# A four-layer graph network on one core: weight splitting regrouped and moved, and a finer alternation in the last stage

## The reference

```
x = layernorm(x + L0(x, edge_attr, src, dst))   # edge MLP: tanh(concat(x[s], x[r]) @ W0 + b0), tanh(. @ W1 + b1),
                                                # . @ W2 + b2, times (edge_attr @ Wg), mean over the edges of s
x = layernorm(x + L1(x, edge_index))            # two GCN convolutions with self loops, relu between them
x = layernorm(x + L2(x, edge_index))            # three SAGE convolutions, relu between them
x = layernorm(x + L3(x, edge_index))            # mean over neighbours of x @ W + b
```

## Time and profile before

| what | value |
|---|---|
| median of 3 runs | 3159.2 us (3157.09 to 3163.51) |
| the profiled execution's own time | 3163.51 us |
| its span, first to last instruction | 3161.9 us |
| mean granted TensorE clock | 0.988 of full speed |
| PE busy | 3050.7 us (96%) |
| DVE, ACT, POOL busy | 2156.2, 1558.9, 1372.1 us |

### The profile page before, as it was taken

The page is one execution under the profiler, slowest core; times in us unless marked ns, Lnnn a source line. Parts: engine busy times, 40 slices in busy tenths (PEclk is TensorE's granted clock), DMA queues, the critical chain, the costliest instruction groups (busy, mean ns, idle before and its releaser), DMA issues. The chain is left out here.

```text
span 3161.9 us, 65361 instructions
## 1 busy us (share of the span) xinstructions
PE 3050.7 (96%) x17338; PEld 2445.7 (77%) x17340; DVE 2156.2 (68%) x5608; ACT 1558.9 (49%) x3158; POOL 1372.1 (43%) x1479
## 2 busy tenths in 40 slices
PE   7699999999999999999998889999999999999899
PEld 7588888888888888888886566667777888887676
DVE  7788888888888888888885777774655222246523
ACT  2466666666666666666664777771111111111344
POOL 2677777777777777777773211220000000000011
PEclk9899999999999999999999999999999999999999
DMA  5555555555555555555553888887556777778586
GB/s 175 170 164 162 161 165 164 164 164 162 162 164 164 164 164 163 165 163 164 164 163 117 262 262 267 276 276 234 171 183 192 231 220 225 218 231 260 99 127 99
DMA packets 298299, 584.82 MB, mean 185 GB/s; under 512 B 43361, under 2 KB 150842, under 8 KB 298234
## 3 DMA queue, kind: packets, MB, share of 16 engines
q1 hardware_dynamic: 180960, 280.20, 29.9%
q0 software_dynamic: 90416, 254.46, 29.2%
q10 hardware_dynamic: 26858, 49.32, 4.3%
HBM read 493.97 MB, written 110.32 MB: 191 GB/s over the span
## 5 line engine op out<-in xcount | busy, mean ns | idle before, releaser
L985 PE MATMUL bank<-parts,ring 128*128 128x512 f32 x2500 | 622.6, 398 | 4.0 <-DVE T_buf L1761 1.9
L985 PEld LDWEIGHTS bank<-parts,ring 128*128 128x128 f32 x2500 | 461.1, 189 | 104.7 <-issue 5.4
L620 POOL DMA_INDIRECT msgs<-rows_out,sidx x416 | 408.4, 982 | 152.0 <-issue 94.8
L613 POOL DMA_INDIRECT p_in<-p_tab,gidx x416 | 403.4, 970 | 138.7 <-issue 112.7
L613 POOL DMA_INDIRECT q_in<-q_tab,gidx x416 | 398.3, 958 | 126.8 <-issue 126.2
L675 PE MATMUL bank<-hidden1h,w1h 128*108 128x512 f32 x936 | 406.8, 435 | 2.3 <-DVE hidden2l L865 2.3
L675 PE MATMUL bank<-w2h,hidden2h 108*128 108x256 f32 x1248 | 402.1, 322 | 0.0
L676 PE MATMUL bank<-hidden1l,w1h 128*108 128x512 f32 x936 | 369.0, 394 | 0.0
L677 PE MATMUL bank<-hidden1h,w1l 128*108 128x512 f32 x936 | 367.7, 393 | 0.0
L784 ACT ACTIVATE hidden2h<-bank,b1c 108x512 fp32r<-108x512 f32 (+1 forms) x312 | 214.5, 688 | 297.8 <-PE bank L691 297.8
L677 PE MATMUL bank<-w2h,hidden2l 108*128 108x256 f32 x1248 | 351.0, 281 | 0.0
(11 more groups left out here) (253 smaller groups left out, 5858.3 us busy)
## 6 DMA issues: line engine op xcount, KB each, us to landing
ring<-counts SPq DMA_DIRECT2D x500, 320.0 KB, 3.4
R_buf<-msgs SPq DMA_DIRECT2D x544, 130.0 KB, 3.1
counts<-cells ACTq DMA_DIRECT2D x125, 320.0 KB, 3.3
eT<-in_edge_T SPq DMA_DIRECT2D x104, 256.0 KB, 2.9
R_buf<-counts POOLq DMA_DIRECT2D x25, 480.0 KB, 6.8
R_buf<-counts POOLq DMA_DIRECT2D x25, 320.0 KB, 5.8
p_in<-p_tab,gidx POOLq DMA_INDIRECT x416, 3.2
q_in<-q_tab,gidx POOLq DMA_INDIRECT x416, 3.2
```

Source lines behind the costliest of these rows:

```text
L613: pool.indirect_dma_start(out=rows_in[:, z, c], out_offset=None, in_=tab[:], in_offset=bass.IndirectOffsetOnAxis(ap=gidx[:, z, which, c:c ...
L620: pool.indirect_dma_start(out=msgs[:], in_=rows_out[:, z, c], in_offset=None, out_offset=bass.IndirectOffsetOnAxis(ap=sidx[:, z, c:c + 1], ...
L985: mm = pe.matmul(bU[t].rearrange("p (w c) -> p w c", w=2), ring[:, cell(odd, a), t * P:(t + 1) * P].bitcast(dt), parts[k % 2][:, :, a].bit ...
```

## The change

It has five parts.

- **W0 is split in one piece.** ACT makes one cast of 128 by 1664 in place of four of 128 by 416, and DVE one subtraction in place of four; DVE no longer has steps of the index chain between them, and TensorE waits for the whole of it ahead of its first matmul.
- **ACT issues the seven loads of W1, W2, Wg and b1 first**, ahead of its wait for W0, where they stood behind the cast of W0 and the rounding of the first two tiles of x.
- **The low parts of W1 and W2** are made on POOL in the table stage, one third behind `xl` of each of tiles 8, 9 and 10 (six instructions), and the 32-row piece of W1 on DVE after tile 15; DVE's three instructions at the head of the edge stage go.
- **TensorE's wait on `s_one`** ahead of its edge loop goes.
- **The last stage alternates one group of turns with one group of products**, where it alternated two with two.

```diff
--- before.py
+++ after.py
@@ -224,6 +224,7 @@
 
                 @block.tensor
                 def _(pe):
+                    pe.wait_ge(s_w0l, 1)
                     pe.wait_ge(s_cg, 5)
 
                     def totals(n):
@@ -259,8 +260,6 @@
                         for half in range(2):
                             for k in range(KD):
                                 to, q = psum[2 * (n % 3) + half][:, 0:H1], 2 * half + k
-                                if n == 0:
-                                    pe.wait_ge(s_w0l, q + 1)
                                 xk_h, xk_l = xh[:, n % 3, k].bitcast(F32R), xl[:, n % 3, k].bitcast(F32R)
                                 pe.matmul(to, xk_h, w0h[:, q].bitcast(F32R), start=(k == 0), stop=False)
                                 pe.matmul(to, xk_h, w0l[:, q].bitcast(F32R), start=False, stop=False)
@@ -296,18 +295,6 @@
 
                 @block.scalar
                 def _(act):
-                    def round_x(n):
-                        act.wait_ge(s_xt[n % TB], 16 * (n // TB + 1))
-                        wait(act, s_pq, n - 2)
-                        wait(act, s_xl, n - 2)
-                        act.copy(xh[:, n % 3].bitcast(F32R), xt[:, n % TB]).then_inc(s_xh, 1)
-
-                    act.wait_ge(s_w, 32)
-                    for q in range(2 * KD):
-                        act.copy(w0h[:, q].bitcast(F32R), w0[:, q]).then_inc(s_w0h, 1)
-                        if q == 0:
-                            round_x(0)
-                    round_x(1)
                     act.dma_start(w1[:, 0:H1F], W1[0:H1F * P, :].rearrange("(k p) n -> p k n", p=P)).then_inc(s_wl, 16)
                     for i in range(3):
                         act.dma_start(w1[i * H1R:(i + 1) * H1R, H1F], W1[H1F * P:H1, :]).then_inc(s_wl, 16)
@@ -315,6 +302,16 @@
                     act.dma_start(wg[:], Wg).then_inc(s_wl, 16)
                     act.dma_start(b1c[:], b1).then_inc(s_wl, 16)
 
+                    def round_x(n):
+                        act.wait_ge(s_xt[n % TB], 16 * (n // TB + 1))
+                        wait(act, s_pq, n - 2)
+                        wait(act, s_xl, n - 2)
+                        act.copy(xh[:, n % 3].bitcast(F32R), xt[:, n % TB]).then_inc(s_xh, 1)
+
+                    act.wait_ge(s_w, 32)
+                    act.copy(w0h[:].bitcast(F32R), w0[:]).then_inc(s_w0h, 1)
+                    round_x(0)
+                    round_x(1)
                     for n in range(T):
                         j = n % TB
                         if n + 2 < T:
@@ -343,11 +340,20 @@
                     pool.iota(iota_s[:], [[1, NST]], base=0, channel_multiplier=0,
                               allow_small_or_imprecise_dtypes=True).then_inc(s_cg, 1)
                     pool.memset(inert[:], -1.0).then_inc(s_cg, 1)
+                    def weights_low(k):
+
+                        pool.wait_ge(s_hi, 3)
+                        stand_alone(pool, s_up)
+                        pool.tensor_tensor(w1l[:, k].bitcast(F32R), w1[:, k], w1h[:, k], ALU.subtract)
+                        pool.tensor_tensor(w2l[:, k].bitcast(F32R), w2[:, k], w2h[:, k], ALU.subtract)
+
                     for n in range(T):
                         pool.wait_ge(s_xh, n + 1)
                         wait(pool, s_pq, n - 2)
                         pool.tensor_tensor(xl[:, n % 3].bitcast(F32R), xt[:, n % TB], xh[:, n % 3], ALU.subtract
                                            ).then_inc(s_xl, 1)
+                        if TB + 3 <= n < TB + 3 + H1F:
+                            weights_low(n - TB - 3)
                     pool.wait_ge(s_cg, 7)
                     pool.wait_ge(s_xl, T)
 
@@ -375,18 +381,10 @@
 
                     ch.link(v.tensor_scalar(qi[:], xf[:], 1.0 / T, -0.48, ALU.mult, ALU.add))
                     ch.link(v.tensor_copy(qf[:], qi[:]))
-
-                    def w0_low(q):
-
-                        v.wait_ge(s_w0h, q + 1)
-                        v.tensor_tensor(w0l[:, q].bitcast(F32R), w0[:, q], w0h[:, q], ALU.subtract).then_inc(s_w0l, 1)
-
-                    w0_low(0)
+                    v.wait_ge(s_w0h, 1)
+                    v.tensor_tensor(w0l[:].bitcast(F32R), w0[:], w0h[:], ALU.subtract).then_inc(s_w0l, 1)
                     ch.link(v.scalar_tensor_tensor(rf[:], qf[:], -float(T), xf[:], ALU.mult, ALU.add))
-                    w0_low(1)
                     ch.link(v.tensor_scalar(mf[:], rf[:], float(T), None, ALU.is_ge))
-                    w0_low(2)
-                    w0_low(3)
                     ch.link(v.tensor_tensor(qf[:], qf[:], mf[:], ALU.add))
                     ch.link(v.scalar_tensor_tensor(rf[:], mf[:], -float(T), rf[:], ALU.mult, ALU.add))
                     ch.link(v.tensor_scalar(mf[:], rf[:], 0.0, None, ALU.is_lt))
@@ -526,6 +524,10 @@
                             shifted(n)
                         if LATE < n < LATE + HN - 2 and (n - LATE) % 2 == 1:
                             record((n - LATE) // 2)
+                        if n == LATE + HN - 2:
+                            mid = slice(H1R, 2 * H1R)
+                            v.wait_ge(s_hi, 3)
+                            v.tensor_tensor(w1h[mid, H1F].bitcast(F32R), w1[mid, H1F], w1h[mid, H1F], ALU.subtract)
                         if n == AT_ROWS:
                             bucket_rows()
                         if n == AT_COLS:
@@ -734,8 +736,6 @@
                     pe.wait_ge(s_took, j + 1)
                     add_to_ranks(t, rest_b, isinstance(j, int) and j == G - 1).then_inc(s_next, 1)
 
-                pe.wait_ge(s_one, 3)
-
                 def body(t):
                     transposes(t, 0)
                     transposes(t, 1)
@@ -923,16 +923,8 @@
                     message(t, 2)
                     message(t, 3)
 
-                def weights_low():
-
-                    mid = slice(H1R, 2 * H1R)
-                    v.tensor_tensor(w1l[:, 0:H1F].bitcast(F32R), w1[:, 0:H1F], w1h[:, 0:H1F], ALU.subtract)
-                    v.tensor_tensor(w1h[mid, H1F].bitcast(F32R), w1[mid, H1F], w1h[mid, H1F], ALU.subtract)
-                    v.tensor_tensor(w2l[:].bitcast(F32R), w2[:], w2h[:], ALU.subtract)
-
                 for z in range(2):
                     table_rows(z, z)
-                weights_low()
                 v.memset(hidden2h[:], 1.0).then_inc(s_one, 1)
                 v.memset(hidden2l[:], 0.0).then_inc(s_one, 1)
                 v.tensor_copy(count_to, iota[:, 0:P]).then_inc(s_one, 1)
@@ -1573,13 +1565,11 @@
                                 tile_step(3, B - 1, *step)
 
                         def body(n, z, use, turns=True, before=range(QN)):
-                            for lead in range(0, QN, 2):
-                                pair = range(lead, min(lead + 2, QN))
-                                for q in pair if turns else []:
+                            for q in range(QN):
+                                if turns:
                                     turn(n, z, use, q)
-                                for q in pair:
-                                    if q in before:
-                                        products(n - 1, 1 - z, q, AT_exact[1 - z], F32R)
+                                if q in before:
+                                    products(n - 1, 1 - z, q, AT_exact[1 - z], F32R)
 
                         left = range(EARLY, QN)
                         body(1, 1, 0, False, left)
```

More of the change, by code:

```diff
@@ L298, in _ @@
                 def _(act):
+                    act.dma_start(w1[:, 0:H1F], W1[0:H1F * P, :].rearrange("(k p) n -> p k n", p=P)).then_inc(s_wl, 16)
+                    for i in range(3):
+                        act.dma_start(w1[i * H1R:(i + 1) * H1R, H1F], W1[H1F * P:H1, :]).then_inc(s_wl, 16)
+                    act.dma_start(w2[:], W2b.rearrange("(k p) n -> p k n", p=H2P)).then_inc(s_wl, 16)
+                    act.dma_start(wg[:], Wg).then_inc(s_wl, 16)
+                    act.dma_start(b1c[:], b1).then_inc(s_wl, 16)
                     def round_x(n):
@@ L305, in _ @@
                     act.wait_ge(s_w, 32)
-                    for q in range(2 * KD):
-                        act.copy(w0h[:, q].bitcast(F32R), w0[:, q]).then_inc(s_w0h, 1)
-                        if q == 0:
-                            round_x(0)
+                    act.copy(w0h[:].bitcast(F32R), w0[:]).then_inc(s_w0h, 1)
+                    round_x(0)
                     round_x(1)
-                    act.dma_start(w1[:, 0:H1F], W1[0:H1F * P, :].rearrange("(k p) n -> p k n", p=P)).then_inc(s_wl, 16)
-                    for i in range(3):
-                        act.dma_start(w1[i * H1R:(i + 1) * H1R, H1F], W1[H1F * P:H1, :]).then_inc(s_wl, 16)
-                    act.dma_start(w2[:], W2b.rearrange("(k p) n -> p k n", p=H2P)).then_inc(s_wl, 16)
-                    act.dma_start(wg[:], Wg).then_inc(s_wl, 16)
-                    act.dma_start(b1c[:], b1).then_inc(s_wl, 16)
                     for n in range(T):
```

## The result

The changed kernel takes 3172.61 us in the median of 6 runs (3168.55 to 3200.93), the kernel before 3156.88 us in 6 runs beside it (3153.74 to 3163.51). The ratio is 1.0054 with a 95% interval of 1.0031 to 1.0078: slower by 15.7 us as the medians stand, by 17 (10 to 25) as the ratio does. The profiled execution took 3170.52 us, its span is 3168.8.

The account below looks back on a forecast made before the run. DVE was taken to bound the table stage up to 30 us, TensorE the last stage. 1.0 + 2.5 + 2.5 + 0.2 + 0 + 4.7 + 0.9 = 11.8 us on 3159.2 gave 3171.0, range 3163 to 3178.

Parts of the forecast that it names:

- W0 in one piece: Table stage start: undivided cast and subtraction make DVE's chain net 1.0 us later, bounds 0 and 1.6.
- loads first: Kernel start: the seven loads, 1.09 MB, compete with W0's transfer and cost 2.5 us, bounds 0 and 3.3.
- low parts on POOL, and the 32-row piece: Table stage: POOL's six instructions hold up DVE's one-hots, 2.5 us (0 to 4.8); the DVE piece adds 0.2 (0 to 0.5).
- head of the edge stage, `s_one`: Edge stage: DVE's saved 2.6 us are off the path, and TensorE's next adds wait behind the same signal; both 0.
- changes of kind in the last stage: Last stage: three more switches between turns and products per row tile, 0.071 us each over 22 tiles, 4.7 us.
- wait on ACT's copy: Last stage: first products nearly wait for ACT's copy of the last group; 0.04 us a tile, 0.9 in all, bounds 0 and 2.
- early terms absorbed: Start and table stage: loads yield to W0, POOL's instructions fall into spare time; 5.9 us stay, 3165.1; chance 0.15.
- The rival that made the kernel faster by it: Edge stage head: DVE's saved 2.6 us show in full, other terms come to nothing; 3156.6 us; chance 0.05.
- No cost of a change of kind: Last stage: switching between turns and products costs nothing in short runs; 6.2 us stay, 3165.4; chance 0.10.
- Dearer start: Start and table stage: loads cost 3.3, POOL's instructions 4.8, half-rate stretch falls worse; 16.9 us, 3176.1 and more; chance 0.15.

Follow-up runs that it names:

- the last experiment: The changed kernel with its last stage put back to two turns, then two products: 3197.05 us for 3184.49 of the kernel before, ratio 1.0045.
- One turn ahead: The kernel before with each last-stage product group placed behind the next group's turn: 3188.05 us, ratio 1.0013 on the third chip.

## Why the prediction was right, and where its terms were off

The forecast of 11.8 us met about 15. That 3171.0 and 3172.61 lie closer than this is luck in part: the kernel before came out at 3156.88 in the later runs, 2.3 us below the 3159.2 that the sum was added to. And the sum came near although one term was five times too small, since others were too large. Its terms, with what the traces and the parts alone measured:

| term | forecast, us | measured, us |
|---|---|---|
| W0 in one piece | 1.0 | 0.8 at tile 0, 0.6 at tile 16 (0 to 5.4 by time) |
| loads first | 2.5 | 1.4 at the cast, 1.3 at tile 16 (-1.3 to 4.4 by time) |
| low parts on POOL, and the 32-row piece | 2.5 + 0.2 | 3.0 to 3.1 and 0.4 where they stand; 5.2 by tile 24 with the half-rate stretches (1.9 to 7.3 by time) |
| head of the edge stage, `s_one` | 0 | 0 (`s_one` was not tried alone) |
| changes of kind in the last stage | 4.7 | 3.6 to 4.0 |
| wait on ACT's copy | 0.9 | 4.4 |

*What bounds.* Right in both stages. Each microsecond that TensorE lost in the last stage was one of the whole: 8.0 in the trace, 8.6 (5.7 to 11.8) in time.

*W0.* The working held to the hundredth (1.60 and 1.90 forecast, 1.58 and 1.89 measured), and about 0.8 arrive at tile 0.

*Loads first.* Sized too large. I let 0.37 of the 1.09 MB fit into the room in the slices (the six slices that I named leave 0.385 MB, and they end at 6.0 us, not 5.4; that is 0.05 us) and then added for W0. The loads issued from 0.9 us on, and the slices from 3.6 to 6.0 us moved 367 to 393 GB/s where they had moved 92 to 288, above the 335 that I had taken as full. So 1.4 of the possible 3.3 us were lost; by an estimate at 330 GB/s about 0.6 MB fitted in. The Trainium skill, "DMA: Bandwidth & Descriptors", section "Issuing engines are not separate DMA queues", says that the DMAs of all issuing engines run on the same 16 DMA engines and interleave. From that I had worked out the 3.3 as the full share; this trace shows 1.4 of it. Rival "early terms absorbed" was right that the loads yield in part, and wrong that the loss is absorbed: the 2.1 us at tile 0 (22.60 against 20.5) stay whole, as the last experiment shows (2.18 at tile 0, 2.06 at tile 24).

*POOL.* The cause was right, the count a little short: 3.0 to 3.1 us for 2.5. I counted six small one-hots and hid a quarter. The large ones were held up as well (1.14 and 1.25 for 0.56), and one small one met two of POOL's instructions in a row (1.62). The Trainium skill, "SBUF — State Buffer", section "SBUF: two separate sides", with its lock on the ports that DVE and GpSimd share, had led to 4.8; the 3.0 to 3.1 lie nearer to my term. The 5.2 by tile 24 hold the 32-row piece, 0.4, and 1.8 us that go, as I read it, with stretches at half rate, which stood in the sum with nothing. That it is the overlap and not the work is shown: the same instructions at 87 us cost nothing measurable.

*Head of the edge stage.* Shown three times: the wait for the gathered rows grew from 0.38 us to 2.95, 2.77 and 2.84, and the addition came no earlier. The rival that made the kernel faster by it falls.

*Changes of kind.* 0.071 us each was forecast; 7.36, 7.49, 7.62 and 7.87 - 0.20 = 7.67 us for row tiles with two, four, six and seven runs of turns give 0.06. A linear cost per change, also in runs of 16.

*The wait on ACT's copy.* The step that failed, and the only one clearly outside its bounds (0 to 2). The prediction has the numbers: copy done 0.53 us after the last turn "plus the signal", product due at 0.57. It then charged 0.04 us, as if the signal were nearly free. In the changed kernel the copy is done 0.54 us after the last turn (2999.51 - 2998.97), and the product starts 0.23 later, so 0.54 + 0.23 - 0.57 = 0.20 a tile and 22 x 0.20 = 4.4 us. One turn ahead removes it, and the stage falls from 203.3 to 197.1. It more than made up for the loads; that the forecast came out near is luck in this.

*Rivals.* "No cost of a change of kind" falls by the tiles with two to seven runs. "Dearer start" was right that half-rate stretches move and cost time: after had one at 79 to 84 us. It was wrong on the loads, and on POOL's instructions by themselves.

## What to carry to other kernels

Where the trace shows an engine without idle time, price a reordering by that engine's own rows, and put a signal's latency into each wait as a number (here 0.23 us from the end of ACT's copy to the product), since twenty-two small ones made half of the stage's loss. Work moved to an engine with room can still hold up another engine while both are busy (one-hots of 0.23 us took up to 1.62); place it where nobody waits for that other. And a gain at a point where the trace names a transfer as the later one is no gain. Before a microsecond is given to an edit, look for a second profile whose half-rate stretches fall in the same places.

## What was not expected of the hardware

*The edge stage has two lengths for the same code.* POOL's mean time for a `p_in` gather between 1010 and 1310 us is 967 or 968 ns in the one and 1,021 to 1,037 in the other; in the second TensorE is idle for about 1% of the time, and the stage takes some 23 to 34 us more (1580 to 1587 us from the first gather to the last, for 1553 to 1557). Windows of 300 us in the kernel before and in the one with the loads first, and POOL's groups in the same windows (count, busy us, mean ns, idle us before):

```profile
1010.00:1310.00 300.00, 300.00 (x1888) 250.78 (x1887) 250.46 (x610) 194.04 (x353) 228.38 (x236) 1.00 0.56 164
...
L613 POOL DMA_INDIRECT p_in<-p_tab,gidx x78 | 75.5, 967 | 23.8 <-issue 21.0 <-PE bank L691 2.7
```

```profile
1010.00:1310.00 300.00, 296.82 (x1845) 243.91 (x1846) 245.15 (x595) 189.97 (x345) 229.91 (x231) 1.00 0.53 160
...
L614 POOL DMA_INDIRECT p_in<-p_tab,gidx x76 | 78.4, 1032 | 23.2 <-issue 22.9 <-PE bank L709 0.3
```

POOL issues 231 DMAs in place of 236, with the usual 0.30 us between them. POOL and TensorE are near to a tie here: in the short form TensorE is busy for all of the 300 us and POOL for 228.4 and 236 x 0.30 = 71, which is 299. So a small slip makes POOL the bound. The four profiles that enter this form stay in it until the stage ends (the one with the loads first from about 400 us on). Three of them are of the third chip's four, which fits the kernel before taking 3184 us there and 3158 on the second.

The traces also show which gathers are the long ones. Timeline of POOL and of DVE in the kernel with the loads first:

```profile
1022.03 1.25 POOL L614 DMA_INDIRECT p_in<-p_tab,gidx  x1 [0.30 <-issue]
```

```profile
1021.89 0.56 DVE L833 TENSOR_TENSOR R_buf<-p_in,q_in 128x384 f32<-128x384 f32 x1
1022.37 0.29 DVE L836 TENSOR_TENSOR R_buf<-p_in,q_in 128x128 f32<-128x128 f32 x1
```

The gather starts 0.14 us behind the start of DVE's additions of gathered rows and ends at 1023.28, 0.62 behind the end of the second one. Between 1010 and 1610 us the four profiles in the longer form have 186 gathers of 1.1 us or more, out of 1225. Every one starts 0.05 to 0.22 us behind the start of such a pair of additions and ends 0.62 to 0.64 behind its end. The profiles in the short form, the kernel before among them, have no gather as long; there none starts that close behind an addition. That points to the additions holding POOL up when the two fall together, and to a rhythm that keeps them together once it has slipped. No run moved them apart, and what makes the rhythm slip is open.

*One chip was 18% slower in the total.* The kernel before on it and on the usual one, windows of the edge stage:

```profile
200.00:1600.00 1400.00, 1190.51 (x6806) 962.43 (x6807) 909.78 (x2202) 694.62 (x1280) 844.62 (x851) 0.93 0.42 127
```

```profile
200.00:1600.00 1400.00, 1400.00 (x8804) 1169.05 (x8803) 1167.99 (x2845) 908.75 (x1651) 1063.90 (x1099) 1.00 0.56 163
```

All engines wait there, and DMA moves 127 GB/s for 163; yet the last stage lasted 195.3 us as elsewhere. Why that chip moves less in the edge stage, no run shows. A part of a kernel can be measured on such a chip if its own stretch of the trace is read.
